# Two stacked depthwise convolutions on one core: border rows kept in three parts, and nine single slots for x with stores in odd and loads in even periods

## The reference

```python
def _gn(v, G=32, eps=1e-05):
    g = v.reshape(B_, G, C_ // G, H_, W_)
    m = jnp.mean(g, axis=(2, 3, 4), keepdims=True)
    s = jnp.var(g, axis=(2, 3, 4), keepdims=True)
    return ((g - m) / jnp.sqrt(s + eps)).reshape(v.shape)
...
# first: channel-wise 1x1, 3x3 and 5x5 kernels, weighted by alpha
    return alpha[0] * x + alpha[1] * out1 + alpha[2] * out3 + alpha[3] * out5
...
    x = x + _L0_conv_ref(_gn(x), L0_conv_w1, L0_conv_w3, L0_conv_w5, L0_conv_alpha)
    x = x + _L1_conv_ref(_gn(x), L1_conv_w, L1_conv_b)   # one 3x3 kernel for all channels, and a bias
```

## Time and profile before

| | |
|---|---|
| median of 3 runs | 431.48 us (428.29 to 431.50) |
| the profiled execution | 432.64 us, of which the span from first to last instruction is 430.8 us |
| granted TensorE clock | 0.903 of full speed |
| busy, VectorE / TensorE / ScalarE / GpSimd | 318.1 / 318.5 / 304.1 / 262.3 us |
| moved by DMA | 69.40 MB, mean 161 GB/s |

### The profile page before, as it was taken

The page is one execution under the profiler, slowest core; times in us unless marked ns, Lnnn a source line. Parts: engine busy times, 40 slices in busy tenths (PEclk is TensorE's granted clock), DMA queues, the critical chain, the costliest instruction groups (busy, mean ns, idle before and its releaser), DMA issues.

```text
span 430.8 us, 12547 instructions
## 1 busy us (share of the span) xinstructions
PE 318.5 (74%) x5206; PEld 276.8 (64%) x5206; DVE 318.1 (74%) x688; ACT 304.1 (71%) x372; POOL 262.3 (61%) x206
## 2 busy tenths in 40 slices
PE   2491586754986998679894998499848989898440
PEld 2361273643986798459883897389836989897220
DVE  7861899971886998399929994889649996779620
ACT  1407257089999699939995899759993999977320
POOL 6405055058788578827885588738882788865601
PEclk9997596995999899969996999889998999999685
DMA  6689488201687769676986788676868514731965
GB/s 151 169 174 204 129 188 169 73 3 41 159 200 164 199 177 210 158 189 202 199 194 171 198 184 202 161 214 173 189 163 223 145 41 118 201 97 28 264 173 146
DMA packets 112829, 69.40 MB, mean 161 GB/s; under 512 B 4540, under 2 KB 109892, under 8 KB 112772
## 3 DMA queue, kind: packets, MB, share of 16 engines
q1 hardware_dynamic: 106088, 65.31, 60.5%
q10 hardware_dynamic: 6684, 3.29, 3.3%
HBM read 41.10 MB, written 27.48 MB: 159 GB/s over the span
## 4 chain that ended last, share of the span: by engine, by line
DVE 33%; DMA 21%; SPq 13%; ACT 13%; PE 9%; issue 4%; ACTq 2%; POOL 2%; POOLq 0%; DVEq 0%
DVE xt L697 15%; DVE stats L641 13%; DMA xt<-in_x_dram 10%; PE ps L377 8%; DMA edge_scratch<-gnX 6%; ACT gn_f L551 5%; SPq L236 5%; ACT gnX L552 4%; ACT cross L561 3%; SPq L216 3%; DMA edge_scratch<-gnY 2%; SPq L250 2%; POOL gnX L864 1%; SPq L263 1%; ACTq L244 1%
## 5 line engine op out<-in xcount | busy, mean ns | idle before, releaser
L377 PE MATMUL ps<-gnX,band 64*64 64x512 f16 x2880 | 181.6, 397 | 29.9 <-DVE xt L697 18.1
L377 PEld LDWEIGHTS ps<-gnX,band 64*64 64x64 f16 x2880 | 161.1, 188 | 46.6 <-issue 40.2
L697 DVE SCALAR_TENSOR_TENSOR xt<-ps,unscale,xt 128x512 f32<-128x512 f32 (+1 forms) x194 | 143.8, 747 | 22.9 <-PE ps L377 20.1
L641 DVE BATCH_NORM_STATS2 stats<-xt 128x6 f32<-128x384 f32 x256 | 120.9, 546 | 45.6 <-DMA xt<-in_x_dram 44.9
L377 PE MATMUL ps<-gnY,band 64*64 64x512 f16 x1728 | 116.8, 414 | 33.7 <-DVE xt L697 33.7
L864 POOL TENSOR_TENSOR gnX<-gn_f,gnX 128x768 f16<-128x768 f32 x60 | 92.7, 1545 | 60.7 <-ACT gnX L552 60.7
L377 PEld LDWEIGHTS ps<-gnY,band 64*64 64x64 f16 x1728 | 97.9, 190 | 49.1 <-ACT gnY L552 23.0
L551 ACT ACTIVATE gn_f<-xt,g_add,g_mul 128x768 f32<-128x768 f32 x120 | 122.1, 1017 | 4.9 <-DVE g_add L681 4.3
L864 POOL TENSOR_TENSOR gnY<-gn_f,gnY 128x768 f16<-128x768 f32 x60 | 92.7, 1545 | 31.0 <-ACT gnY L552 31.0
L561 ACT ACTIVATE cross<-ps,unscale 64x512 f32<-64x512 f32 x94 | 64.2, 683 | 51.0 <-PE ps L377 49.4
L873 POOL TENSOR_TENSOR xt<-xt,cross 128x512 f32<-128x512 f32 x47 | 61.7, 1315 | 57.3 <-ACT cross L561 57.2
(11 more groups left out here) (78 smaller groups left out, 97.9 us busy)
## 6 DMA issues: line engine op xcount, KB each, us to landing
out_dram<-xt SPq DMA_DIRECT2D x56, 384.0 KB, 4.8
xt<-in_x_dram SPq DMA_DIRECT2D x48, 384.0 KB, 6.4
band<-diag_scratch SPq DMA_DIRECT2D x48, 160.0 KB, 3.0
haloX<-edge_scratch SPq DMA_DIRECT2D x32, 123.4 KB
xt<-in_x_dram SPq DMA_DIRECT2D x20, 192.0 KB, 4.3
xt<-in_x_dram ACTq DMA_DIRECT2D x12, 192.0 KB, 6.0
out_dram<-xt SPq DMA_DIRECT2D x12, 192.0 KB, 4.0
haloX<-edge_scratch SPq DMA_DIRECT2D x32, 61.7 KB
```

Of the source, the lines that this page charges most:

```text
L377: mm = nc.tensor.matmul(ps[to, c, half, :], weights(rows, half), moving(rows, half), start=first, stop=last)
L641: st = nc.vector.bn_stats(stats[:, q_of(at, i) % 2, at, b, e, :], flat[:, SUB * e:SUB * (e + 1)])
L697: ev = nc.vector.scalar_tensor_tensor(out=here, in0=ps[frm, c, half, :].rearrange("h (b w) -> h b w", b=NB), scalar=unscale[rows, at:at + ...
```

## The change

**Borders.** `edges_out` writes the high part a second time, as a third part of the scratch, with a transfer of its own beside each one that was there: 8 writes in place of 4 for X, 4 in place of 2 for Y. `edges_in` reads all three parts in one transfer per half: 2 reads in place of 4, for X and for Y. The same bytes are read; half as many again are written.

**Slots.** `xt` has nine slots of one unit. Channels 0 to 47 lie in the lower partitions and 48 to 95 in the upper ones, so that any two neighbouring units are contiguous. Units are stored in odd periods (unit 0 alone in period 3, then units j - 4 and j - 3 together, at the end 13, 14 and 15 alone) and loaded in even periods (units j + 4 and j + 5 in period j; units 4 and 5 still in period 1). Two units whose slots are 8 and 0 are loaded apart. The `stored` semaphores are now one for each batch.

**Room.** `cross` has two slots in place of three, used in turn, and `halo_w` for X overlaps its zeros, from 6144 to 3230 elements per partition.

```diff
-    NX = 4
+    NX = 9
+    PRE = 4
...
-        edge_dram = [nc.dram_tensor(f"edge_scratch{s}", [2, 2, 2, 2, FAR[s], ROW], fp16, kind="Internal").ap() for s in (X, Y)]
+        edge_dram = [nc.dram_tensor(f"edge_scratch{s}", [2, 2, 3, 2, FAR[s], ROW], fp16, kind="Internal").ap() for s in (X, Y)]
...
-        halo_w = [sb("halo_wX", [P, NU * CG, 2, R], fp16), sb("halo_wY", [P, 2, R], fp16)]
+        halo_w = [sb("halo_wX", [P, NU * CG * (R + FAR[0]) + R - FAR[0]], fp16), sb("halo_wY", [P, 2, R], fp16)]
...
-        xt = sb("xt", [P, NX, NB, 2, CG, 2, W])
+        xt = sb("xt", [P, NB, NX, CG, 2, W])
...
-        cross = sb("cross", [P, NCROSS, NB, W])
+        cross = sb("cross", [P, 2, NB, W])
...
-            return 4 * CG * (i // 2) + 2 * CG * g + CG * (i % 2)
+            return C // 2 * g + CG * i
...
-                        eng.dma_start(edge_dram[s][p, g, :, side, :, :].rearrange("h r e -> r h e"), src).then_inc(edges_landed[s], 16)
+                        eng.dma_start(edge_dram[s][p, g, 0:2, side, :, :].rearrange("h r e -> r h e"), src).then_inc(edges_landed[s], 16)
+                        eng.dma_start(edge_dram[s][p, g, 2, side, :, :], src[:, 0, :]).then_inc(edges_landed[s], 16)
...
+                    eng.dma_start(edge_dram[s][p, :, 2, side, 0, :],
+                                  bass.AP(src.tensor, src.offset, [[R * pitch, 2], [1, ROW]])).then_inc(edges_landed[s], 16)
...
-                for at, parts in ((0, 2), (2, 1)):
-                    eng.dma_start(halo[s][R * g + at * n:R * g + (at + parts) * n, p, :, :, :]
-                                  .rearrange("r b c w -> r (b c w)")[:, 0:EDGE],
-                                  bass.AP(src.tensor, src.offset + taps[0], [[ROW, parts * rows], [1, len(taps)], [1, EDGE]]))\
-                       .then_inc(halo_in[s][p], 16)
+                eng.dma_start(halo[s][R * g:R * g + n, p, :, :, :].rearrange("r b c w -> r (b c w)")[:, 0:EDGE],
+                              bass.AP(src.tensor, src.offset + taps[0], [[ROW, 3 * rows], [1, len(taps)], [1, EDGE]]))\
+                   .then_inc(halo_in[s][p], 16)
...
+        def joint(n):
+
+            return n % NX + 1 < NX
...
+            def stores_in(j):
+
+                if j < LAG + 1:
+                    return None
+                if j == LAG + 1 or j >= NU:
+                    return j - LAG - 1, 1
+                return (j - LAG - 2, 2) if j % 2 else None
+
+            def loads_in(j):
+
+                if j == 1:
+                    return PRE
+                return j + PRE if j % 2 == 0 and 2 <= j < NU - PRE else None
...
-                if i >= 1:
-                    act.wait_ge(cross_added, NCROSS * (i - 1) + min(c, NCROSS - 1) + 1)
+                k = crosses_before(i, c)
+                if k >= 2:
+                    act.wait_ge(cross_added, k - 1)
```

More of the change, by code:

```diff
@@ L193, in crossed_to, with crosses_before @@
             return sum(crossed(n, c) for n in range(i + 1) for c in range(CG))
+        def crosses_before(i, c):
+            return crossed_to(i - 1) + sum(crossed(i, k) for k in range(c))
         def halo_landed(n):
-            return 64 * (n // 2 + 1)
+            return 32 * (n // 2 + 1)
         def split(s, i):
@@ new lines, in images, with rows_of, loaded @@
+        def images(t, n, g, b, units):
+            c = first_channel(n, g)
+            return t[b, c:c + units * CG, :, :].rearrange("c (e p) w -> p (c e) w", e=2)
+        def rows_of(n, g, b, units):
+            at = n % NX
+            return xt[HALVES[g], b, at:at + units, :, :, :].rearrange("p u c e w -> p (u c e) w")
+        def joint(n):
+            return n % NX + 1 < NX
+        def loaded(n):
+            return sum(128 if joint(k) else 256 for k in range(PRE, n + 1, 2) if (k - n) % 4 == 0)
@@ L242, in load_unit, with load, store @@
+        def load(eng, n, b, units, done):
             for g in range(2):
[L243 to L247, removed]
+                eng.dma_start(rows_of(n, g, b, units), images(x, n, g, b, units)).then_inc(done, 16)
+        def store(eng, n, b, units):
@@ L248, in load_pair @@
             for g in range(2):
[L249 to L258, removed]
@@ L260, in store_pair @@
-        def store_pair(eng, m, b):
-            for g in range(2):
-                c = first_channel(2 * m, g)
-                eng.dma_start(out[b, c:c + 2 * CG, :, :].rearrange("c (e p) w -> p (c e) w", e=2),
-                              xt[HALVES[g], m % NX, b, :, :, :, :].rearrange("p u c e w -> p (u c e) w"))\
-                   .then_inc(stored[m % NX], 16)
+                eng.dma_start(images(out, n, g, b, units), rows_of(n, g, b, units)).then_inc(stored[b], 16)
         @block.sync
@@ L364, in _ @@
             for b in (0, 1):
-                store_unit(sp, LAST, b)
-            for r in range(NX):
-                sp.wait_ge(stored[r], 256 if r < NX - 1 else 384)
+                store(sp, LAST, b, 1)
+            for b in range(NB):
+                sp.wait_ge(stored[b], 32 * (stores_until(LAST) + 1))
         @block.tensor
@@ L869, in cross_add @@
             def cross_add(i, c):
-                pool.wait_ge(cross_out, crossed_to(i - 1) + sum(crossed(i, k) for k in range(c + 1)))
+                k = crosses_before(i, c)
+                pool.wait_ge(cross_out, k + 1)
                 here = x_of(i)[:, :, c, 1, :]
-                nc.gpsimd.tensor_tensor(here, here, cross[:, c, :, :], ALU.add).then_inc(cross_added, 1)
+                nc.gpsimd.tensor_tensor(here, here, cross[:, k % 2, :, :], ALU.add).then_inc(cross_added, 1)
             mid = diag[:, R - 1 - PAD:R + PAD, :][:, ::-1, :]
```

66 lines of the change are left out of this document (35 added, 31 removed).

## The result

The change makes the kernel 1% slower: 434.82 us (median of 12 runs, 431.78 to 436.66) against 431.01 for the kernel before (12 runs); the ratio is 1.0101, with a 95% interval of 1.0071 to 1.0131. The profiled execution took 435.95 us. Each pad line in a kernel makes them one higher. The profiled executions of runs 1, 2, 7, 11 and 16 took 3.5 to 4.9 us more than the medians of their kernels, so a stretch read from one of these traces can be too long by up to that much.

What follows compares the result with a forecast made beforehand. Late x loads stalled VectorE; SyncE's queue was to bound next. Profiled 432.6 - 16.8 - 1.8 - 2.0 - 3.5 - 0.6 = 407.9 us, median 406.7, given as 407; range 390 to 419.

Steps and rivals of the forecast that it cites:

- Edits at no cost: Two slots of cross, the channel map and the new layouts of xt and halo_wX: no time lost.
- Loads a period earlier: In the middle, loading x a period sooner removes all five VectorE waits on x, 34.7 us.
- SyncE's queue becomes the bound: In the middle, SyncE's queue takes 42.0 us per pair of periods, against 46.2 before and ScalarE's 38.4.
- The holes: Idle gaps in SyncE's queue: 3.6 us before the X read shrinks by 1.1; 1.6 us of Y-border waiting returns.
- The middle: Eight periods: four pairs gain 4.2 us each, 16.8 in all, plus 1.8 us of margin used up once.
- The start and the end: Shorter zeroing of halo_wX gains 0.6 us; storing units 11 and 12 earlier gains 3.5; the first pair gains 2.0.
- C: Rival, slower: SyncE's queue grows to 52.5 us a pair through dearer writes and longer landings; 450 us; chance 0.05.
- A: Rival, full relief: holes in SyncE's queue close and ScalarE bounds at 38.4 us a pair; 392.6 us; chance 0.26.
- B: Rival, smaller gain: each third-part write costs 0.56 us, a pair takes 44.7; 419 us; chance 0.16.

Runs made afterwards that it cites:

- run 1: The changed kernel with the old edges_out and edges_in, so the new slots without the new borders; 446.27 us, ratio 1.0363.
- run 2: The kernel before with only the new borders (scratch of three parts, one read per half); 421.87 us, ratio 0.9807.
- run 7: The kernel before with the new borders, cross in two slots and the overlapped halo_wX; 438.80 us, ratio 1.0169.
- run 11: The new slots with the old borders, and 192 unused bytes ahead of xt so it is aligned; 420.97 us, ratio 0.9796.
- run 16: The changed kernel with xt aligned, with ScalarE issuing the Y border writes in place of SyncE; 408.59 us, ratio 0.9513.
- run 9: The kernel before with only xt moved to 64 bytes past a multiple of 256; 455.39 us, ratio 1.0594.
- run 12: The kernel before with only xt moved to 128 bytes past a multiple of 256; 442.41 us, ratio 1.0277.
- run 14: The kernel before with xt at an odd multiple of 256 bytes; 429.59 us, ratio 0.9978.
- run 8: The whole changed kernel with 192 unused bytes ahead of xt, so xt begins at a multiple of 256; 413.54 us, ratio 0.9631.
- run 15: The aligned changed kernel without the third part's border writes from unit 2 on (part of the computation left out); 396.93 us, ratio 0.9215.
- run 10: The kernel before with the new borders, cross in two slots, the overlapped halo_wX and 192 unused bytes ahead of xt; 419.20 us, ratio 0.9768.
- run 3: The changed kernel, xt not aligned, without the third part's border writes from unit 2 on; 419.75 us, ratio 0.9742.
- run 17: The aligned changed kernel with GpSimd issuing the Y border writes, all but the last unit's; 415.72 us, ratio 0.9637.

## Why the prediction was wrong, step by step

**The step that failed** is the one called "Edits at no cost": "The channel map, the new layout of `xt` and of `halo_wX` leave every operation's size as it was." That is true of sizes and says nothing of places. The shorter `halo_wX` moved `xt` to 64 bytes past a multiple of 256, and the 92,160 rows of 512 bytes that SyncE's queue moves in and out of it took (286.0 - 260.6) x 16 / 92,160 = 4.4 ns longer each (run 9), where a packet takes 260.6 x 16 / 106,088 = 39 ns of an engine on the mean. With the place mended, the same change takes 413.5 us, inside the range of 390 to 419, and the place costs 4.7% of the time before (0.9631 against 1.0101). This is shown both ways: it comes with one pad in the kernel before and goes with one in the changed kernel. The Trainium skill, "DMA: Bandwidth & Descriptors", section "How a descriptor splits into AXI transactions", says that a transaction must begin at a multiple of 256 bytes; worked out from it, a 512-byte row that starts elsewhere needs three transactions in place of two. Runs 9, 12 and 14 agree on the multiple. Counted in beats of 32 bytes as the page counts them, an estimate, 128 bytes off would be dearer than 64 (20 beats against 18, aligned 16), and here it is the other way round, 279.5 against 286.0 us; the measurement decides, and why is open.

**Loads a period earlier: all five waits gone.** Right. What is left of VectorE's waits lies before 80 us.

**SyncE's queue becomes the bound.** The mechanism was right, the size off even when aligned. In the changed kernel as made a pair took 48.4 us; aligned, 180.3 / 4 = 45.1, against 42.0 forecast. The traced pair of run 8, from 236.31 to 282.12 us, takes 45.8 and shows where:

```profile
242.04 1.61 SPq L244 DMA_DIRECT2D haloY<-edge_scratch  x2
243.75 4.39 SPq L272 DMA_DIRECT2D out_dram<-xt  x4
...
254.25 2.76 SPq L244 DMA_DIRECT2D haloX<-edge_scratch  x2
...
266.23 2.14 SPq L244 DMA_DIRECT2D haloY<-edge_scratch  x2
...
278.98 1.65 SPq L244 DMA_DIRECT2D haloX<-edge_scratch  x2
```

The eight reads take 8.2 us; I had halved 11.9 and taken off 5.9, as if a read of three parts cost what one of two or one did. It costs 0.8 us in place of 0.66, and more behind stores: 2.2 us too little. The third Y write costs 0.51, not 0.3: 0.9 too little for four. The third X write was right at 0.26. Behind stores border writes slow down: the eight X writes take 4.5 us there against 2.9 behind loads, the four Y writes 3.9 against 2.3. All X writes of the pair take 7.4 us where 6.5 stood in the sum, all Y writes 6.2 where 4.6 did. With 2.2 for the reads, and 0.9 less than before for weights and x, this gives the 3.8 us from 42.0 to 45.8. The holes were as counted (2.6 us aligned for the X landing, where 3.6 less 1.1 stood in the sum, and 1.5 for the Y landing against 1.6).

What the third writes add to a pair was put at 3.4 less 1.7 us; without them it was 11.3 / 4 = 2.8 us shorter (run 15 against run 8).

**The middle.** 16.8 and 1.8 us were forecast; aligned it gave 184.9 - 180.3 = 4.6, and the parts say from what. The eight periods of run 10 (borders and room, old slots, aligned) and of run 8, which adds the new slots:

```profile
146.63:328.01 181.38, 152.23 (x2565) 135.70 (x2562) 144.31 (x305) 154.60 (x185) 129.06 (x89) 0.93 0.78 193
```
```profile
145.95:326.21 180.26, 151.82 (x2560) 125.86 (x2564) 144.01 (x303) 152.84 (x183) 127.67 (x88) 0.95 0.70 180
```

And those of the borders alone, and of the slots alone, aligned:

```profile
154.71:334.40 179.69, 152.26 (x2568) 134.16 (x2565) 144.15 (x305) 154.55 (x185) 128.97 (x89) 0.93 0.78 194
```
```profile
150.87:336.59 185.72, 155.68 (x2560) 126.52 (x2564) 143.96 (x303) 150.58 (x180) 125.75 (x87) 0.93 0.70 173
```

The lead of a period takes VectorE's waits on x from 33.2 us in run 10 to 3.9 in run 8, and gives 1.1 us in the middle. In their place stand waits for the X halo, 23.0 us in run 8 and 0.4 in run 10; in the slots alone, aligned, they are 29.2 us, in nine places. The rhythm changed from some 26 and 20 to 24 and 23, with nearly the same sum: 184.9 us before, 185.7 in the slots alone, and that in an execution 3.8 us above the median of its kernel.

**The start and the end.** Start: 2.0 and 0.6 were forecast, 9.3 came aligned (155.2 to 145.95), 8.1 of it by TensorE's first X halo (46.77 to 38.69; in the changed kernel as made it was at 42.70). Run 10, with the room and the borders but the old slots, has that halo at 38.07 and the borders alone at 46.3, so it comes with the room, the shorter zeroing or the two slots of `cross`; the two weren't tried apart. The chain of waits of run 8 begins with the first load of x and has no zeroing in it, where that of before began with it. If it is the zeroing, I had costed it by its own 1.2 us and not by what starts behind it. End: 3.5 forecast, 3.2 in the changed kernel and 4.8 aligned, though the last wait is still 3.10 us; the sum is right and my way to it wasn't shown. It comes with the new slots: from run 10 to run 8 the end shrinks from 90.5 to 85.9 us.

That the aligned change lies inside the range is therefore in part luck: 18.6 us were forecast for the middle and 4.7 came, 2.6 for the start and 9.3 came, 3.5 for the end and 4.8 came.

**The rivals.** C named the right side and the right threshold: it "decides from 48 us a pair", with four landings 1.5 us longer; two are longer, by 1.5 and 1.0 us (3.0 us of hole against 1.5 aligned, and 3.6 against 2.6). But the third part isn't what lengthens them: with the same third writes they are shorter in run 8, and run 3 has fewer writes and the same 286.8 us of busy transfers. A fell with the holes, which did not close even when aligned, and with the reads' price. B's price for a Y write (0.56) was nearer than mine, its 0.56 for an X write (0.26) was not, and its 419 is about as near to the aligned change (5.5 us above) as my 407 (6.5 below).

**Chances.** 0.9 on faster had no place for a tile that moves. The numbers to see it, 6144 and 3230 elements of 2 bytes, stood in the text of the change.

## What to carry to other kernels

When a change resizes any tile, work out where the tiles behind it begin: one of which rows of 512 bytes are transferred should begin at a multiple of 256 bytes, and a pad of 192 bytes was worth 5% here. Busy share times span of a transfer queue, with packets and bytes beside it, shows such a loss in one line; a slower time with that product unchanged is another matter. Waits that were removed from one engine gave next to no time here, since the queue that feeds the next one had none to spare. An issue that is moved to relieve it should be moved only in the stretch where that queue binds.

## What was not expected of the hardware

A transfer's cost per 512-byte row depends on the offset of its on-chip side: 260 us of busy transfers at multiples of 256 (an odd one as good as an even one), 279.5 at 128 past, 286.0 at 64 past. Other tiles may be off without a cost that could be measured (412.95 against 413.54 us), and so may the engines' operands. X border writes, from two neighbouring partitions, issue in 0.26 us (medians), with two parts or with one. Y border writes of the same bytes, from two partitions 64 apart, take 0.56 us with two parts and 0.51 with one. GpSimd issues the latter kind in 0.56 to 0.57 us (run 17), ScalarE in 0.51 to 0.52 (run 16).
